# Split pairs gated first on GpSimd, with product and high and low parts in PSUM, three up banks and one accumulator

## The reference, cut to what matters

```python
router_probs = softmax(x @ router_w.T + bias)        # 64 experts
topk_p, topk_i = top_k(router_probs, 6)              # normalised to sum 1: the gates
hg = einsum('ecd,efd->ecf', expert_in, w_gate)       # F = 64 per expert, D = 128
hu = einsum('ecd,efd->ecf', expert_in, w_up)
expert_out = einsum('ecf,edf->ecd', silu(hg) * hu, w_down)
out = shared_out / 2 + sum over experts of gate * expert_out   # two shared experts
```

## Time and profile before

| | |
|---|---|
| three timed runs | 716.76, 717.83, 718.17 us; median 717.83 |
| profiled execution | span 716.0 us, first to last instruction; no other time is given for it |
| PE busy | 692.8 us, 97% of the span, 3133 matmuls |
| PEld busy | 524.7 us, 73% |
| DVE busy | 523.4 us, 73% |
| POOL busy | 466.5 us, 65% |
| ACT busy | 350.6 us, 49% |
| chain that ended last | PE 88%, DVE 4%, issue 3%, POOL 2%, ACT 1% |

### The profile page before, as it was taken

One profiled execution on the slowest core, in us unless ns is written; L12 is line 12 of the kernel. 1 busy time (PEld: TensorE's weight loads), 2 busy tenths in 40 slices (PEclk: granted clock), 3 DMA queues, 4 the chain that ended last, 5 costly groups with the idle time before them and its releaser, 6 DMA issues.

```text
span 716.0 us, 9975 instructions
## 1 busy us (share of the span) xinstructions
PE 692.8 (97%) x3133; PEld 524.7 (73%) x3133; DVE 523.4 (73%) x1074; ACT 350.6 (49%) x609; POOL 466.5 (65%) x345
## 2 busy tenths in 40 slices
PE   7788899999999999999999999999999999999998
PEld 7666677777777777777777777777777777777775
DVE  5677686987768867887769877788678766674444
ACT  3543455446454374445553474544745435534432
POOL 5035477776677767685676776676775656676664
PEclk9999999999999999999999999999999999999999
DMA  5504232243323333333333433333333433334431
GB/s 204 226 1 128 71 118 104 85 133 105 111 106 114 114 108 99 120 113 102 118 103 101 128 103 103 118 110 109 114 105 102 125 103 105 115 112 124 138 123 60
DMA packets 48869, 80.17 MB, mean 112 GB/s; under 512 B 9520, under 2 KB 13744, under 8 KB 48816
## 3 DMA queue, kind: packets, MB, share of 16 engines
q1 hardware_dynamic: 47792, 77.44, 33.4%
q0 software_dynamic: 1024, 2.10, 1.2%
HBM read 76.35 MB, written 3.15 MB: 111 GB/s over the span
## 4 chain that ended last, share of the span: by engine, by line
PE 88%; DVE 4%; issue 3%; POOL 2%; ACT 1%; DVEq 0%; POOLq 0%
PE bank_y L467 16%; PE bank_g L481 8%; PE bank_g L482 8%; PE bank_g L483 8%; PE bank_u L483 8%; PE bank_u L481 8%; PE bank_u L482 8%; PE bank_y L464 4%; PE bank_y L462 4%; PE bank_y L461 4%; POOL hid L1040 1%; PE bank_f L408 1%; PE bank_f L386 1%; PE bank_f L402 1%; PE bank_f L445 1%
## 5 line engine op out<-in xcount | busy, mean ns | idle before, releaser
L1040 POOL TENSOR_TENSOR hid<-hid,gate_rows 128x512 f32<-128x512 f32 x256 | 374.2, 1470 | 195.4 <-DVE hid L881 193.0
L623 ACT ACTIVATE hid<-bank_g 128x512 f32<-128x512 f32 x264 | 156.6, 599 | 264.4 <-PE bank_g L483 261.8
L881 DVE TENSOR_TENSOR hid<-hid,bank_u 128x512 f32<-128x512 f32 x264 | 178.7, 681 | 128.3 <-PE bank_u L483 78.2
L481 PE MATMUL bank_g<-x_hi,gate_hi 128*128 128x512 f32 x264 | 142.9, 541 | 0.0
L467 PE MATMUL bank_y<-hid,w_down 128*128 128x512 f32 x272 | 138.7, 591 | 0.0
L887 DVE TENSOR_TENSOR hid_lo<-hid,hid_hi 128x512 fp32r<-128x512 f32 x128 | 110.2, 861 | 2.4 <-ACT hid_hi L629 2.4
L482 PE MATMUL bank_g<-x_hi,gate_lo 128*128 128x512 f32 x264 | 104.5, 396 | 0.0
L483 PE MATMUL bank_g<-x_lo,gate_hi 128*128 128x512 f32 x264 | 104.5, 396 | 0.0
L481 PE MATMUL bank_u<-x_hi,up_hi 128*128 128x512 f32 x264 | 103.9, 393 | 0.1
L483 PE MATMUL bank_u<-x_lo,up_hi 128*128 128x512 f32 x264 | 103.8, 393 | 0.0
L482 PE MATMUL bank_u<-x_hi,up_lo 128*128 128x512 f32 x264 | 103.8, 393 | 0.0
(11 more groups left out here) (209 smaller groups left out, 857.1 us busy)
## 6 DMA issues: line engine op xcount, KB each, us to landing
gate_rows<-gates_dram SPq DMA_DIRECT2D x512, 128.0 KB, 2.9
w_down<-down_t_dram SPq DMA_DIRECT2D x3, 704.0 KB, 14.5
out_dram<-later SPq DMA_DIRECT2D x7, 256.0 KB, 3.1
hid<-gate_t_dram SPq DMA_DIRECT2D x2, 704.0 KB, 5.8
gates_dram<-gates_t SPq DMA_DIRECT2D x8, 128.0 KB, 2.2
gate_rows<-up_t_dram SPq DMA_DIRECT2D x1, 704.0 KB, 5.7
later<-up_t_dram SPq DMA_DIRECT2D x1, 704.0 KB, 9.9
raw<-gate_t_dram SPq DMA_DIRECT2D x1, 704.0 KB, 11.0
```

What stands on the lines that cost most here:

```text
L481: pe.matmul(o, w_hi[name][:, p, :], x3_hi[par][:, :], start=True, stop=False)
L623: act.activation(hid[:, slot(par, p), :], bank_g[(p + par) % 2][:, :], ACT.Silu).then_inc(sem("silu"), 1)
L881: dve.tensor_tensor(hid[:, s, :], hid[:, s, :], bank_u[(p + par) % 2][:, :], ALU.mult)\
L1040: pool.tensor_tensor(hid[:, s, :], hid[:, s, :], gate_rows[:, row, :], ALU.mult)\
```

## The change

The number of split pairs stays 16, but the list is another: plain are 0 to 4, the even ones from 6 to 20, and 24, 26, 28, 30; split are 5, 7, 9, 11, 13, 15, 17, 19, 21, 22, 23, 25, 27, 29, 31, 32. The order of a split pair's steps is changed: GpSimd multiplies the gate row into `hid` right after the silu; VectorE then multiplies by the up bank and leaves the product in that bank (`dve_product`, one iteration after the pair's matmuls); ScalarE copies the high part from the bank (`act_hi`, one iteration later too, after that iteration's silu); VectorE subtracts, bank minus `hid_hi` (`dve_lo`, two iterations later). Both VectorE steps now stand at the head of the iteration (`dve_split`), ahead of the batch's other work. Plain pairs go as before.

The up bank of a split pair is free when its `dve_lo` is done. There are three up banks, in turn, and one accumulator, so the first `down` of a batch waits for the copy of the last one, which moves from iteration 5 to 4. `hid_hi` and `hid_lo` have three buffers each. `down_hi` and `down_lo` are made run by run of neighbouring split pairs: 13 instructions each in place of one. `ones_row`, `decay_full` and `vals` lose their own space (a column read with step 0, a slice of `x1`, and `xn2_t` stand in).

```diff
-SPLIT_LAG, SPLIT_RING = 2, 2
-SPLITS = PAIRS // 2
+SPLIT_RING = 3
+PLAIN_PAIRS = (0, 1, 2, 3, 4, 6, 8, 10, 12, 14, 16, 18, 20, 24, 26, 28, 30)
+SPLIT_PAIRS = tuple(p for p in range(PAIRS) if p not in PLAIN_PAIRS)
+SPLITS, PLAINS = len(SPLIT_PAIRS), len(PLAIN_PAIRS)
...
-        bank_u = [bank(f"bank_u{i}") for i in range(2)]
-        bank_y = [bank(f"bank_y{i}") for i in range(2)]
+        bank_u = [bank(f"bank_u{i}") for i in range(3)]
+        bank_y = bank("bank_y")
...
# down
+            if p == 0:
+                wait(pe, "ffn_t", b)
...
# gate_up
-                wait(pe, freed, q - 1)
-                o = banks[ring][:, :]
+                if name == "gate":
+                    wait(pe, "silu", q - 1)
+                else:
+                    b3, p3 = pairs_back(b, p, 3)
+                    if b3 is not None and is_split(p3):
+                        pe.wait_ge(sem("hid_lo"), split_count(b3, p3))
+                    elif b3 is not None:
+                        pe.wait_ge(sem("up_used"), plain_count(b3, p3))
...
-        def act_hi(act, b, par, p):
-            q = PAIRS * b + p
-            act.wait_ge(sem("gated"), q + 1)
-            wait(act, "down_done", q - 2 * SPLIT_RING + 1)
-            act.activation(hid_hi[:, (p // 2) % SPLIT_RING, :], hid[:, slot(par, p), :], ACT.Copy)\
+        def act_hi(act, b, p):
+            act.wait_ge(sem("product"), split_count(b, p))
+            wait(act, "down_done", split_slot_freed(b, p))
+            act.activation(hid_hi[:, split_slot(b, p), :], bank_u[(PAIRS * b + p) % 3][:, :], ACT.Copy)\
                .then_inc(sem("hid_hi"), 1)
...
# start, ScalarE
-                    act.activation(down_hi[:, :, :], odd_pairs(w_down), ACT.Copy).then_inc(sem("down_hi"), 1)
+                    for j, pairs in split_runs():
+                        last = act.activation(down_hi[:, j, :], w_down[:, pairs, :], ACT.Copy)
+                    last.then_inc(sem("down_hi"), 1)
...
-        def dve_lo(dve, b, par, p):
-            k = (p // 2) % SPLIT_RING
+        def dve_product(dve, b, p):
+            q = PAIRS * b + p
+            dve.wait_ge(sem("gated"), q + 1)
+            dve.wait_ge(sem("pe_up"), q + 1)
+            u = bank_u[q % 3][:, :]
+            dve.tensor_tensor(u, hid[:, slot(b % 2, p), :], u, ALU.mult).then_inc(sem("product"), 1)
+
+        def dve_lo(dve, b, p):
+            k = split_slot(b, p)
             dve.wait_ge(sem("hid_hi"), split_count(b, p))
-            dve.tensor_tensor(hid_lo[:, k, :], hid[:, slot(par, p), :], hid_hi[:, k, :].bitcast(F32), ALU.subtract)\
-               .then_inc(sem("hid_lo"), 1)
+            dve.tensor_tensor(hid_lo[:, k, :], bank_u[(PAIRS * b + p) % 3][:, :], hid_hi[:, k, :].bitcast(F32),
+                              ALU.subtract).then_inc(sem("hid_lo"), 1)
+
+        def dve_split(dve, b, p):
+            b2, p2 = pairs_back(b, p, 2)
+            if b2 is not None and is_split(p2):
+                dve_lo(dve, b2, p2)
+            b1, p1 = pairs_back(b, p, 1)
+            if b1 is not None and is_split(p1):
+                dve_product(dve, b1, p1)
...
             for p in range(PAIRS):
+                dve_split(dve, b, p)
...
-                if p >= AHEAD - 1 or not first:
+                if (p >= AHEAD - 1 or not first) and not is_split(p):
                     dve_up(dve, b, par, p)
-                if p >= SPLIT_LAG and is_split(p - SPLIT_LAG):
-                    dve_lo(dve, b, par, p - SPLIT_LAG)
...
# GpSimd
-                pool.wait_ge(sem("up_used"), q + 1)
+                if is_split(p):
+                    pool.wait_ge(sem("silu"), q + 1)
+                else:
+                    pool.wait_ge(sem("up_used"), plain_count(b, p))
```

More of the change, by code:

```diff
@@ L281, in split_lo @@
                 dve.wait_ge(sem("down_hi"), 1)
[L282 to L283 removed]
+                for j, p in split_runs():
+                    last = dve.tensor_tensor(down_lo[:, j, :], w_down[:, p, :], down_hi[:, j, :].bitcast(F32),
+                                             ALU.subtract)
+                last.then_inc(sem("down_lo"), 1)
         def gate_row_loads(sp, b, r):
@@ L463, in down @@
                 pe.wait_ge(sem("hid_lo"), split_count(b, p))
-                pe.matmul(y, down_hi[:, j, :], hid_lo[:, k, :], start=False, stop=False).then_inc(sem("down_done"), 1)
+                pe.matmul(y, down_hi[:, j, :], hid_lo[:, k, :], start=False, stop=(p == PAIRS - 1)).then_inc(sem("down_done"), 1)
             else:
@@ L475, in gate_up @@
                     pe.wait_ge(sem(f"split_lo{CHUNK_OF[n, p]}"), 1)
-            ring = (p + par) % 2
-            for name, banks, freed in (("gate", bank_g, "silu"), ("up", bank_u, "up_used")):
-                wait(pe, freed, q - 1)
-                o = banks[ring][:, :]
+            if b == 0 and p == 2:
+                pe.wait_ge(sem("h"), 2)
+            for name, o in (("gate", bank_g[q % 2][:, :]), ("up", bank_u[q % 3][:, :])):
+                if name == "gate":
[6 more added lines that the diff above has]
+                        pe.wait_ge(sem("up_used"), plain_count(b3, p3))
                 pe.matmul(o, w_hi[name][:, p, :], x3_hi[par][:, :], start=True, stop=False)
@@ L647, in act_sequence @@
                 act_silu(act, b, par, p)
-                if p >= SPLIT_LAG and is_split(p - SPLIT_LAG):
-                    act_hi(act, b, par, p - SPLIT_LAG)
-                elif not first and p < SPLIT_LAG and is_split(p - SPLIT_LAG + PAIRS):
-                    act_hi(act, b - 1, 1 - par, p - SPLIT_LAG + PAIRS)
+                b1, p1 = pairs_back(b, p, 1)
+                if b1 is not None and is_split(p1):
+                    act_hi(act, b1, p1)
         def split_hi(act, at):
@@ L681, in _ @@
             last = BATCHES - 1
-            for p in range(PAIRS - SPLIT_LAG, PAIRS):
-                if is_split(p):
-                    act_hi(act, last, 1, p)
+            if is_split(PAIRS - 1):
+                act_hi(act, last, PAIRS - 1)
             act.wait_ge(sem("down_done"), PAIRS * BATCHES)
@@ L982, in _ @@
             last = BATCHES - 1
-            for p in range(PAIRS - SPLIT_LAG, PAIRS):
-                if is_split(p):
-                    dve_lo(dve, last, 1, p)
+            dve_split(dve, last, PAIRS)
+            if is_split(PAIRS - 1):
+                dve_lo(dve, last, PAIRS - 1)
             dve.wait_ge(sem("stored"), 16 * BATCHES)
```

73 lines of the change are left out of this document (45 added, 28 removed).

## The result

The changed kernel takes 748.9 us (median; 747.99 to 752.2), the kernel before 718.0 (716.76 to 719.84): a ratio of 1.0437, 95% interval 1.0409 to 1.0465. The forecast was 740, its own range 730 to 748, and 717 to 754 the range that should hold 8 in 10. The change cost 31 us and not 22: the loop between VectorE and GpSimd came as forecast, and a second loss came that the forecast didn't have. The wide range holds the result only because its upper end was drawn from F1, the falling clock, which didn't happen. The profiled execution took 749.16 us with a span of 747.4 (before: span 716.0).

A forecast was written before the change was run, and what follows sets the result against it. TensorE was taken as the bound, busy 82.54 of 83.03 us a batch. 16.8 + 2.1 + 2.0 + 1.1 = 22.0 us on a 716.0 span, plus 1.8 for timed runs, gave 740; range 730 to 748, 8-in-10 range 717 to 754.

The forecast's parts named there:

- F1: Rival: the granted clock falls at PE's new waits, one fall a batch, 13 us more, 753 us; chance 0.17.
- A: DVE-POOL loop beside the router: PE waits for up banks before pairs 26, 28, 30; 2.4 us a batch, 16.8 in all.
- B: Gates after pair 27's low part in iteration 29 come late: 0.3 us a batch, 2.1 in all.
- C: Iteration 6: pair 5's product delays the scores, PE's wait 0.49 becomes 0.9; 2.0 us over five batches.
- D: Start: thirteen copies on ScalarE in place of one of 1.90 us; half of +2.4 taken, 1.1 us.
- E: What costs nothing: freed accumulator, third ring slots, smaller constants, moved act_hi, last pair; batch-0 hole left at 0.
- hidden steps: Freed accumulator with its earlier copy, third ring slots, smaller constants, moved act_hi: no engine waits on them, 0 us.
- F2: Rival: the loop is shorter, one of three waits left, about 0.8 us a batch, 727 us; chance 0.17.
- F3: Rival, faster: the product finds its gating done, no bank late, iteration-6 waits and batch-0 hole go, 711 us; chance 0.11.

The follow-up runs named there:

- e1: The changed kernel with VectorE's product moved behind the other work of its iteration, the low part staying at the head: 736.87 us.
- e4: The changed kernel with GpSimd multiplying only the first half of each pair's columns by the gate row: 719.65 us.
- u1: The changed kernel with the split pairs' steps and what hangs on them back in the old order, high and low part made from SBUF: 715.39 us.
- e5: e3 with the product written to hid in SBUF, so the up bank is free with the product, not the low part: 768.01 us.
- e2: The changed kernel with VectorE's four xn2 instructions moved from iteration 11 to 10: 741.07 us.
- u2: u1 with the old list of split pairs (all odd ones) and one copy at the start: 718.22 us.
- e3: The changed kernel with both the product moved later, as in e1, and xn2 moved sooner, as in e2: 728.38 us.
- u3: u1 with down_hi and down_lo made in 4 instructions each, over pairs a fixed step apart, in place of 13: 714.46 us.
- d19: Old order, new list with three more split pairs (12, 14, 20), xn2 in iteration 10, six strided copies at the start: 715.72 us.

## Why the prediction was right, and where its size was off

**A, the loop, was right step by step.** PE's up matmuls in iterations 25 to 30 and the transposes of the gates:

```profile
388.27 0.40 PE L524 MATMUL bank_u<-x_hi,up_hi 128*128 128x512 f32 x1
...
390.88 0.50 PE L524 MATMUL bank_u<-x_hi,up_hi 128*128 128x512 f32 x1 [0.35 <-DVE hid_lo L938]
...
395.81 0.50 PE L524 MATMUL bank_u<-x_hi,up_hi 128*128 128x512 f32 x1 [0.50 <-DVE hid_lo L938]
...
401.08 0.50 PE L524 MATMUL bank_u<-x_hi,up_hi 128*128 128x512 f32 x1 [0.69 <-DVE hid_lo L938]
...
403.53 0.65 PE L462 MATMUL bank_f<-ident,turns 128*128 128x128 f32 x4 [0.63 <-DVE turns L862]
```

From start to start that is 2.61, 4.93 and 5.27 us. Before it was 2.09 (372.65 to 374.74), 4.34 and 4.32: PE loses 0.52 before pair 26 (0.51 forecast), 0.59 before 28 (0.68 to 1.12) and 0.95 before 30 (1.0 to 1.09), together 2.06 where 2.4 was taken. (The batch shown is the worst: in the others PE waits 0.47 to 0.51 before 30 and not 0.69.) The row of before that the first distance starts from:

```profile
372.65 0.40 PE L481 MATMUL bank_u<-x_hi,up_hi 128*128 128x512 f32 x1
```

The start of the chain came as forecast too: the silu of pair 24 begins 2.90 us after PE's up matmuls of that pair (386.01 to 388.91), before 2.56 (370.42 to 372.98), so 0.34 later. Against the batch's start it is 2.2 later, since PE itself has lost xn2's 1.5 us by then (below). VectorE's half of the loop:

```profile
389.54 0.69 DVE L924 TENSOR_TENSOR hid<-hid,bank_u 128x512 f32<-128x512 f32 x1 [2.39 <-ACT hid L666]
...
392.87 0.70 DVE L933 TENSOR_TENSOR bank_u<-hid,bank_u 128x512 f32<-128x512 f32 x1 [2.04 <-POOL hid L1100]
...
394.48 0.68 DVE L924 TENSOR_TENSOR hid<-hid,bank_u 128x512 f32<-128x512 f32 x1
...
396.52 1.25 DVE L846 TENSOR_SCALAR tstat<-tstat 128x4 f32<-128x4 f32 x1
397.78 0.69 DVE L933 TENSOR_TENSOR bank_u<-hid,bank_u 128x512 f32<-128x512 f32 x1
...
399.74 0.69 DVE L924 TENSOR_TENSOR hid<-hid,bank_u 128x512 f32<-128x512 f32 x1
```

and GpSimd's, plain and split pair in one run of 2.5 us:

```profile
390.30 2.53 POOL L1100 TENSOR_TENSOR hid<-hid,gate_rows 128x512 f32<-128x512 f32 x2 [5.12 <-DVE hid L924]
395.23 2.51 POOL L1100 TENSOR_TENSOR hid<-hid,gate_rows 128x512 f32<-128x512 f32 x2 [2.40 <-DVE hid L924]
```

From plain multiply to plain multiply: 394.48 - 389.54 = 4.94, where 4.02 and 1.0 to 1.44 of probabilities were forecast; then 5.26, where 4.02 and 1.3 to 1.39 were. Only in the first round does VectorE stand idle ahead of the product (2.04). In the second there is no idle time: an instruction of the best eight, L846, takes 1.25 us (0.63 before, there L803) and ends at 397.77, with GpSimd's run (397.74), and the product starts behind it. e1 and e4 confirm the cause: with the product out of the way, or GpSimd quicker, the waits shrink or go. The choice of 1.30 over 1.47 for GpSimd held too (1297 ns), and u1 and e5 show why: with the low part's operands in SBUF the multiply is 1474 and 1436. The Trainium skill, SBUF — State Buffer, § SBUF: two separate sides, has a GpSimd instruction and a VectorE one with two SBUF inputs shut each other out of one port pair; by it the product and the low part in PSUM are free of that, and the trace agrees (691 and 686 ns in after, 1337 in e5).

**B, the gates, was too small.** From the up matmuls of pair 30 to the transposes of the gates PE takes 2.45 us, before 1.54 (383.40 to 384.94): 0.91 a batch where 0.3 was taken. It lies within the bounds (0 to 1.5). Here too a VectorE instruction with its operands in SBUF lies beside GpSimd's run (400.50 to 403.18): L858 takes 1.12 us, 0.41 before (there L815), and the forecast counted only the next one (L819, now L862) as stretched.

```profile
400.94 1.12 DVE L858 TENSOR_TENSOR turns<-prob,tstat 128x256 f32<-128x256 f32 x1
```

**The term that was missing: xn2, 1.5 us a batch.** Iteration 12 of the same batch, in the timeline of all engines:

```profile
352.48 0.68 DVE L938 TENSOR_TENSOR hid_lo<-bank_u,hid_hi 128x512 fp32r<-128x512 f32 x1
352.64 2.53 POOL L1100 TENSOR_TENSOR hid<-hid,gate_rows 128x512 f32<-128x512 f32 x2 [2.17 <-DVE hid L924]
353.08 3.59 DVE L789 TENSOR_SCALAR xn<-shared,inv 128x128 f32<-128x128 f32 x4
...
355.12 1.27 POOL L1070 TENSOR_TENSOR shared<-emb,shared 128x512 f32<-128x512 f32 x1
...
356.72 0.66 PE L431 MATMUL bank_f<-ident,xn 128*128 128x128 f32 x4 [1.31 <-DVE xn L789]
```

In before these transposes started 0.86 us after the matmul ahead of them (340.37 to 341.23), here 2.33 (354.39 to 356.72):

```profile
341.23 0.60 PE L396 MATMUL bank_f<-ident,xn 128*128 128x128 f32 x4
```

The forecast followed the split pairs through the router's stretch alone. Here, after two table loads on ScalarE, the same meeting happens: the silu comes late, GpSimd then has the plain and the split pair in hand at once, and the four xn2 instructions, which read and write SBUF, take 3.59 us instead of the 0.87 which they take undisturbed (e2 in one batch). Section A asked who waits for VectorE, and not which of VectorE's instructions work on SBUF while GpSimd runs without a pause. e2 shows the term by taking it away, 1.55 a batch, and e4 that GpSimd is what holds them: with its multiplies halved an xn2 instruction takes 585 ns. The term is paid in batches 0 to 5; in batch 6 it is 0.4.

**C had the wrong sign, and was nothing in the end.** Before the state matmuls PE waits 0.30 us in this batch, not 0.9; it had been 0.49. Two effects lie over one another: with the old list and no product (u2) PE waits about 0.4 there, with the new list and no product (u1) not at all. So the list takes the wait away, which the forecast named and didn't price, and the product puts 0.30 back. Of the 0.19 gained nothing is left by pair 12, where PE is level with before to 0.1 us: the list also makes pairs 1 and 3 plain, and their longer `down` falls into these iterations.

**D, the start.** The 13 copies take 3.01 us instead of 1.90, the 1.1 that was taken. That the number fits is luck: it was taken as half of an upper bound of 2.4.

```profile
35.14 3.01 ACT L719 ACTIVATE down_hi<-w_down 128x128 fp32r<-128x128 f32 x13
```

The other 1.5 us of the later first batch lie ahead of the copies, which begin at 35.14 and not at 33.64, and go with TensorE's clock: 0.69 between 10 and 20 us, where before had 1.00. That is the execution's, not the change's: the same stretch, with the same code, has 1.00 in e2, e3, u1 and u3 and 0.83 in e1, where the copies begin at 33.68 to 33.80, and 0.66 to 0.69 in e4, d19, e5 and u2, where they begin at 34.85 to 35.13. From the end of the copies to the first batch it is 22.1 us in before and after alike.

**E, the batch-0 hole.** It was left at 0 and stayed, 2.61 us instead of 2.24. Yet the batch lost 2.0 us and not 4.6, since less of it ran at a low clock. In before it holds two such stretches, 0.66 between 60 and 65 us and 0.72 between 72 and 78. In after the first lies partly ahead of batch 0 (0.81 between 55 and 60, 0.85 between 60 and 65) and the second didn't come (below). The hidden steps cost nothing, as forecast: u2, with three banks, one accumulator and the early copy, is level with before. That pairs 1 and 3 as plain ones would have shrunk the hole without the product of pair 5 (to nothing in u1, to 1.34 us in u3, with the same order and list) was only a bound of this term.

Added up along the starts of PE's up matmuls in the batch shown, against the same ones before: 0.1 us up to pair 12, 1.5 at 13 (xn2), 0.1 up to 25, then 0.5 by 26, 0.6 by 28, 1.0 by 30 and 1.0 by 31 (the gates), which is the whole 4.7 of this batch. Over seven batches A's 16.8 us were about 13, B's 2.1 about 7, C's 2.0 nothing, and xn2 some 10 that the forecast didn't have.

Of the rivals, F1 (the clock falls at the new waits) is refuted: waits of 0.35 to 0.69 us, and the clock is 1.00 in the six batches behind batch 0, and 0.99 in batch 0, whose low stretch between 60 and 65 us comes before the first of them. F2 would have left one wait of three; three are there. F3's condition, that VectorE finds its gating done, is met in no run: ahead of pair 25's product it stands idle 2.04 us in after and still 0.94 in e4. There the banks come in time all the same, but for 0.5 us a batch on a weight load.

**Left open:** the last 1.47 us a batch of e3. By PE's up matmuls it lies wholly in iterations 26 to 31, 0.5 of it at the gates, and VectorE's L846 and L858 take 1.10 and 0.95 us there, in u1 0.63 and 0.41; whether these two are the cause is not shown. Half the gating removes most of it, but halves both the loop and the time in which GpSimd holds the port, so it doesn't tell the two apart; e5 was meant to and brought a greater loss.

## What to carry to other kernels

When two engines each hold one end of a chain, measure the round trip from one instruction of a kind to the next and compare it with the bound's own pace for the same iterations; averages of busy time (65 of 83 us here) say nothing about it. An instruction that must wait for a slow engine is better placed at the end of its iteration's work than at its head: here that gave back 12 of the 31 us (e1). And when GpSimd's work is bunched into runs, look through all of VectorE's SBUF instructions that now fall beside such a run, in every stretch and not only in the one that was changed for.

## What the runs showed of the hardware

Beside a run of GpSimd instructions, VectorE's SBUF instructions got through one at a time. The four xn2 instructions beside the three GpSimd ones (352.64 to 356.39) took 930, 1317, 1300 and 273 ns: the first three ended at 354.01, 355.25 and 356.47, each 0.08 us after a GpSimd instruction had (353.93, 355.17, 356.39), and the fourth came behind the run. All seven batches with xn2 beside the pairs show these durations to 15 ns. The four together lost 2.7 us, while GpSimd's own time stayed at 1.27 to 1.29 an instruction. Where the VectorE instruction has two inputs in SBUF, as e5's low part, GpSimd's time grows as well (1436 ns on the mean). An operand in PSUM costs VectorE nothing that these rows show: 680 to 691 ns with PSUM inputs and outputs, and 0.68 us for u1's low part from SBUF in 99 of 128 cases. The Trainium skill, Perfetto Trace Analysis, § Optimizing Scalar/DVE Operations, puts about 65 ns between the two; the measurement decides.

A hole doesn't always bring the clock down. After 2.24 us of idle PE, before ran at 0.72; after 2.61 us in the changed kernel the stretch was at 1.00:

```profile
76.48 0.91 PE L413 MATMUL bank_f<-z,shared 128*128 128x128 f32 x6 [2.61 <-issue]
```

```profile
72.00:80.00 8.00, 5.39 (x26) 3.66 (x25) 6.57 (x10) 2.11 (x5) 2.47 (x3) 1.00 0.38 114
```

(columns as in the earlier trace rows), and so it was in u2 after 2.42 us. The forecast's fall of the clock rested on one such hole.
